# A fused attention and feed-forward kernel on one core: how the second half's four groups of keys are summed in the front attention

## What is computed

```python
B, S, E, H, P = ...          # 4, 1024, 128, 16, 256 here
scores = jnp.einsum('bhid,bhjd->bhij', q, k)
rel = jnp.einsum('bhid,pd->bhip', q, rel_key)
bias = jnp.take_along_axis(rel, jnp.broadcast_to(rel_idx[None, None], (b, h, s, s)), axis=3)
logits = jnp.where(causal[None, None], (scores + bias) * scale, -jnp.inf)
attn = jax.nn.softmax(logits, axis=-1)
out = jnp.einsum('bhij,bhjd->bhid', attn, v)
```

## Time and profile before

| what | value |
|---|---|
| median of 3 runs | 4309.09 us |
| profiled execution, its own time | 4309.43 us |
| its span, first to last instruction | 4307.6 us |
| mean granted clock of TensorE | 0.977 of full speed |
| busy share PE / DVE / ACT / POOL | 96% / 82% / 85% / 56% |
| PE matmul instructions | 44016 |
| steady part of the front attention | about 130 us to 910 us, one head every 12.58 us |

### The profile page before, as it was taken

One profiled execution on the slowest core, in us unless ns is written; L12 is line 12 of the kernel. 1 busy time (PEld: TensorE's weight loads), 2 busy tenths in 40 slices (PEclk: granted clock), 3 DMA queues, 4 the chain that ended last, 5 costly groups with the idle time before them and its releaser, 6 DMA issues. The chain is left out here.

```text
span 4307.6 us, 124384 instructions
## 1 busy us (share of the span) xinstructions
PE 4136.7 (96%) x44016; PEld 2959.0 (69%) x44016; DVE 3537.9 (82%) x8236; ACT 3655.4 (85%) x6994; POOL 2391.7 (56%) x2876
## 2 busy tenths in 40 slices
PE   4999999997999999999999999999999999999995
PEld 2566666654777777777777777777777777777774
DVE  4788888866888888888888888888888888888884
ACT  4899999966888888888888888888888888888885
POOL 3000000026676766767767777677776776766763
PEclk7999999988999999999999999999999999999997
DMA  6777777731111111111111111111111111111111
GB/s 179 226 229 233 228 234 227 237 128 40 36 42 47 42 37 43 42 47 42 36 44 42 45 43 36 44 42 42 47 36 44 42 42 47 36 41 45 42 47 51
DMA packets 249884, 347.66 MB, mean 81 GB/s; under 512 B 45120, under 2 KB 206508, under 8 KB 249260
## 3 DMA queue, kind: packets, MB, share of 16 engines
q1 hardware_dynamic: 249388, 341.00, 26.6%
HBM read 151.13 MB, written 82.85 MB: 54 GB/s over the span
## 5 line engine op out<-in xcount | busy, mean ns | idle before, releaser
L1459 PE MATMUL la_ps<-la_Wqkv,la_xsT 128*128 128x512 f32 x2304 | 1191.0, 612 | 3.4 <-DVE X L1175 2.8
L1175 DVE TENSOR_TENSOR X<-la_ps,la_tab 128x1024 f32<-128x1024 f32 x768 | 919.9, 1218 | 100.2 <-ACT la_sq L1317 97.1
L1122 POOL TENSOR_TENSOR la_rt<-la_rt,la_rn 128x1024 f32<-128x1024 f32 x384 | 722.3, 1902 | 27.5
L1105 POOL TENSOR_TENSOR la_rt<-X 128x512 f32<-128x512 f32 x384 | 494.9, 1289 | 263.0 <-PE la_ps L1474 165.8
L1182 DVE TENSOR_REDUCE la_ssum<-la_sq 128x8 f32<-128x512 f32 x768 | 502.4, 674 | 0.0
L1106 POOL TENSOR_TENSOR la_rt<-X 128x512 f32<-128x512 f32 x384 | 497.2, 1295 | 0.0
L1494 PEld LDWEIGHTS la_ps<-la_kT,la_qB 128*64 128x64 f32 x12288 | 390.5, 138 | 145.8 <-issue 145.8
L1317 ACT ACTIVATE la_sq<-la_ps 128x512 f32<-128x512 f32 x768 | 448.7, 596 | 45.1 <-PE la_ps L1459 30.5
L1459 PEld LDWEIGHTS la_ps<-la_Wqkv,la_xsT 128*128 128x128 f32 x2304 | 377.0, 190 | 142.8 <-issue 93.7
L528 POOL COPY at_vh<-V 128x64 f32 (+1 forms) x64 | 15.1, 236 | 784.5 <-PE at_ps L727 783.3
L1525 PEld LDWEIGHTS la_ps<-la_Wo,la_oT 128*128 128x128 f32 x3072 | 366.6, 192 | 110.4 <-issue 101.2
(11 more groups left out here) (204 smaller groups left out, 9524.7 us busy)
## 6 DMA issues: line engine op xcount, KB each, us to landing
at_band<-skew_scratch SPq DMA_DIRECT2D x64, 1536.0 KB, 7.3
la_vs<-la_v SPq DMA_DIRECT2D x192, 384.0 KB, 3.5
skew_scratch<-at_R SPq DMA_DIRECT2D x64, 1024.0 KB, 6.6
la_vs<-la_v SPq DMA_DIRECT2D x192, 128.0 KB, 3.4
la_Wqkv<-in_wqkv SPq DMA_DIRECT2D x28, 384.0 KB, 3.7
at_qh<-qt_scratch SPq DMA_DIRECT2D x64, 144.0 KB
at_kh<-kt_scratch SPq DMA_DIRECT2D x64, 144.0 KB
la_W<-in_L_ffn_W SPq DMA_DIRECT2D x24, 341.0 KB, 3.7
```

The source lines that it names most:

```text
L1105: e.tensor_tensor(dst[:, :, 0, :], c[:, :, 0, :], s[:, :, 1, :], ALU.add)
L1122: e.tensor_tensor(heads(rt, w), heads(rt, w), wide(rn[:, w * H:(w + 1) * H], D), ALU.mult)\
L1175: e.tensor_tensor(dst.rearrange("p f (h d) -> p f h d", d=D), ps[:, c % 2, :].rearrange("p (h d) -> p h d", d=D).unsqueeze(1).to_broadcast ...
L1459: e.matmul(ps[:, c % 2, :], xsT[:, m * P:(m + 1) * P], Wqkv[:, ds(layer(n) % 2, 1), c * 512:(c + 1) * 512], start=True, stop=True)\
```

## The change

In the second half (u = 1) `gather` no longer multiplies with `sel`. It makes four plain 128x128 transposes of `part` into bank 7, so that each query has its four strips side by side on its own partition. `over_sum` for u = 1 begins with a VectorE reduction that adds the four strips from PSUM (128 x 36 sums of four) into a new SBUF tile `total`. The reciprocal waits for the reduction and reads `total`, and so does the multiplication. The mark `on` is now raised by the reduction, and the multiplication raises a new one, `c_tot`, for which nobody waits. The first half (u = 0) does what it did.

```diff
-        rc, cell = t.sb("rc", [P, G]), t.sb("cell", [P, TB])
+        rc, cell, total = t.sb("rc", [P, G]), t.sb("cell", [P, TB]), t.sb("total", [P, G, D_A + 1])
...
-        c_on = t.mark("co", JJ)
+        c_on, c_tot = t.mark("co", JJ), t.mark("ct")
...
             def over_sum(n, m, u):
-                o = ps[:, O_BANK, 0:G * (D_A + 1)].rearrange("p (i d) -> p i d", i=G)
+                tile, col = n // H_A * TB + G * u, n % H_A * D_A
+                out = O[:, ds(tile, G), ds(col, D_A)]
                 e.wait_ge(g_mm.sem, g_mm.v(n, u + 1))
-                e.reciprocal(rc[:].unsqueeze(2), o[:, :, D_A:D_A + 1]).then_inc(c_on.sem, 1)
-                e.wait_ge(c_on.sem, c_on.v(n, u + 1))
-                tile, col = n // H_A * TB + G * u, n % H_A * D_A
-                e.tensor_tensor(O[:, ds(tile, G), ds(col, D_A)], o[:, :, 0:D_A], wide(rc[:], D_A), ALU.mult)\
-                    .then_inc(on.sem, 1)
+                if u == 0:
+                    o = ps[:, O_BANK, 0:G * (D_A + 1)].rearrange("p (i d) -> p i d", i=G)
+                    e.reciprocal(rc[:].unsqueeze(2), o[:, :, D_A:D_A + 1]).then_inc(c_on.sem, 1)
+                    e.wait_ge(c_on.sem, c_on.v(n, 1))
+                    e.tensor_tensor(out, o[:, :, 0:D_A], wide(rc[:], D_A), ALU.mult).then_inc(on.sem, 1)
+                else:
+
+                    groups = ps[:, O_BANK, :].rearrange("p (i c d) -> p i d c", i=G, c=G)[:, :, 0:D_A + 1, :]
+                    e.tensor_reduce(total[:], groups, AX.X, ALU.add).then_inc(on.sem, 1)
+                    e.wait_ge(on.sem, on.v(n))
+                    e.reciprocal(rc[:].unsqueeze(2), total[:, :, D_A:D_A + 1]).then_inc(c_on.sem, 1)
+                    e.wait_ge(c_on.sem, c_on.v(n))
+                    e.tensor_tensor(out, total[:, :, 0:D_A], wide(rc[:], D_A), ALU.mult).then_inc(c_tot.sem, 1)
...
             def gather(n, m, u):
                 e.wait_ge(o_ev.sem, o_ev.v(n, u + 1))
                 for i in range(G):
-                    k = WIN * min(G, G * u + i + 1)
-                    mm = e.matmul(ps[:, O_BANK, i * (D_A + 1):(i + 1) * (D_A + 1)],
-                                  part[0:k, i * P:(i + 1) * P], sel[0:k, :], start=True, stop=True)
+                    if u == 0:
+
+                        k = WIN * (i + 1)
+                        mm = e.matmul(ps[:, O_BANK, i * (D_A + 1):(i + 1) * (D_A + 1)],
+                                      part[0:k, i * P:(i + 1) * P], sel[0:k, :], start=True, stop=True)
+                    else:
+                        mm = e.transpose(ps[:, O_BANK, i * P:(i + 1) * P], part[:, i * P:(i + 1) * P], ident[:])
                 mm.then_inc(g_mm.sem, 1)
```

## The result

The changed kernel takes 4331.32 us (median of four runs, 4327.58 to 4332.62), the kernel before 4309.46 us beside it: 21.9 us more, a ratio of 1.0050 with a 95% interval of 1.0038 to 1.0062. The profiled execution took 4332.29 us of its own, with a span of 4330.5 us.

What follows compares the result with a forecast made beforehand. The prediction took the chain `scores(7)`, DVE, `values(0)` as the bound, not PE's 98.5%. The DVE chain grows by 0.31 + 0.05 = 0.36 us, times 61 heads 22 us: 4309.1 + 22 = 4331 us, 8-in-10 range 4319 to 4349.

Steps and rivals of the forecast that it cites:

- The median: Whole kernel: 4331 us forecast, 0.5% slower than before; chance 0.77.
- What bounds: Each head: PE work from `values(0)` to `scores(7)`, about 10 us, plus a DVE chain of 2.4 us.
- PE's saving counted at nothing: `gather(1)`, 0.81 to 0.44 us: the 0.37 us saved per head is lost waiting at `rel(2)` and `values(0)`.
- The reduction: DVE chain before the reciprocal: 144 elements from PSUM take 0.31 us, bounds 0.29 and 0.69.
- The wait on itself: DVE, reciprocal waiting for the reduction: 0.05 us, with 0.24 as other end; free by the skill page.
- Reciprocal and multiplication: DVE, behind the reduction: reading SBUF in place of PSUM, both counted as unchanged.
- The number of heads: Of 64 heads, 61 counted because the first few are less regular; 61 x 0.36 = 22 us.
- no slack waits there to take up the delay: Behind `values(0)` or `least(0)` on PE, DVE and ACT: nothing absorbs the 0.36 us per head.
- PE as the bound: Rival: PE's saved 0.37 us per head counts, kernel gets faster by up to 23 us, 4286 us; chance 0.05.
- something takes up the delay: Rival: ACT or DVE is last later in the head, leaving under 0.14 us per head, say 4312 us; chance 0.07.
- A dear stride: Rival, reduction or its wait costs more: badly read stride 0.69 us, 0.74 per head with short wait, 4354 us; chance 0.10.
- the rival of the falling clock: Rival: transposes replacing products drop PE's clock to 1.2 GHz, some 700 us longer, about 5000 us; chance 0.01.

Runs made afterwards that it cites:

- transposes-only run: Changed kernel without the reduction: reciprocal and multiplication read the first of four strips from PSUM; 4305.6 us beside 4306.1 for the kernel before, ratio 0.9998.
- the two kernels with the loads first: Kernel before and changed kernel, each with query and key loads issued ahead of the band's load on SP: 4296.6 us (0.9976) and 4324.8 us (1.0038).
- reduction-only run: Kernel before, products kept, plus the reduction over bank 7 into unused `total` and a wait for it: 4334.5 us beside 4306.1, ratio 1.0059.

## Why the prediction was right

**The median** was forecast as 4331 and is 4331.3 us. The mechanism is the one that was forecast; that the two numbers agree within 1 us is in part luck, as the number of heads shows below.

**What bounds.** The prediction took the chain `scores(7)`, DVE, `values(0)` for the path and PE's 98.5% for no bound. The two halves of the change, each alone, show it: taking work from PE beside the chain gave a ratio of 0.9998, and adding the reduction to the chain alone gave the changed kernel's head.

**PE's saving counted at nothing.** Right, and the place where it is lost was named: `rel(2)`, waiting for ACT's copy. The size of the saving, 0.37 us, was met (0.81 to 0.43 or 0.44). What the prediction did not see is that a little of it can cover the waits for loads: 2.6 us in the trace of the transposes-only run.

**The reduction.** 0.31 us forecast, 303 ns measured. **The wait on itself.** 0.05 us forecast; 521.11 - (520.78 + 0.303) = 0.03 us measured. By the Trainium skill ("VectorE: DVE Perf Modes", The DRAIN you can't avoid), where a semaphore after each operation costs nothing extra, the prediction would have said 4328. The times alone do not decide between the two, since the executions lie between 4327.58 and 4332.62; the traces speak against the page here, since by the estimate above the instruction that waits starts 0.11 us later than one that does not. The prediction took the end of one record as the earliest start of the next, but records can overlap by 0.08 us, in its own rows too: `least(7)` ends at 512.08 + 0.62 = 512.70, and the reciprocal starts at 512.62. Its sum is not touched by this, because it counted the length of the reduction plus the gap behind it. **Reciprocal and multiplication** out of SBUF take 178 and 192 ns, as out of PSUM. Together 0.34 us against 0.36.

**The number of heads.** 61 times 0.36 us made 22. In detail it was 63 heads and other terms: 63 x 0.336 = 21.2 us, and 1.6 us for a pause that every fourth head pays (15 x 0.11), together 22.8, which the two kernels with the loads first confirm (22.9). Between the kernels as they are the stage grew by only 818.7 - 799.5 = 19.2 us, since the kernel before spent about 3.7 us more on waits for loads, which longer heads cover (799.5 - 795.0 = 4.5 before, 818.7 - 817.9 = 0.8 after). That no slack waits there to take up the delay was thus not quite true. The span of the profiled executions grew by 22.9 us: 3.8 us more are behind the stage, in code that the change did not touch, and the stage began 0.2 us earlier. Over all kernels of the table this rest lies between 3388.5 and 3397.9 us, with no order that I can name. It stays open, and it means that the last few microseconds of the agreement are luck: the same change between the two kernels with the loads first made 4324.8 - 4296.6 = 28 us of the medians.

**The rivals.** PE as the bound fell with the transposes-only run. That something takes up the delay is true for 3.7 of 22.9 us, far from the whole, and it was the waits for loads and not ACT. A dear stride fell with 303 ns. The granted clock stayed at 1.00 in the changed kernel with 40 transposes a head, so the rival of the falling clock fell too. By the Trainium skill ("TensorE: Matmul & The Clock Gate", Part 4: PE-mode transpose), where transposes do not count as busy for the clock in the same way, four more of them would speak for a fall. None came here, and the only trace whose clock fell inside the stage, the reduction-only run's, is of a kernel that kept its products. That transposes count for less than products is neither shown nor ruled out by this, since products ran beside them in every head.

## What to carry to other kernels

An engine that is 98.5% busy need not be the bound: look for the place where it waits once per turn, and for the place where the engine it waits for waits in turn. Here work added between these two places cost its full length, and work saved beside them gave next to nothing, so read the two halves of such a trade separately. When a change frees a buffer earlier, move what no longer has to stand before the release out of the chain; here this turned 22 us lost into 11 us gained. And try a second change on the kernel before as well: the order of the loads looked like the next bound behind that gain, but it gave some 10 us to the kernel before too.

## What the runs showed of the hardware

**The granted clock fell in two heads of one trace.** In the run with the reduction only, the granted clock fell twice inside the stage. PE's row where it fell the first time, then a stretch around the second time and PE's rows there:

```profile
276.82 1.80 PE L731 MATMUL at_ps<-at_pT,at_vh 128*32 128x512 f32 x8 [0.63 <-DVE at_pT L565]
...
690.00:695.00 5.00, 4.38 (x31) 2.25 (x29) 3.40 (x15) 4.64 (x9) 0.18 (x1) 0.84 0.33 67
...
693.38 1.91 PE L731 MATMUL at_ps<-at_pT,at_vh 128*32 128x512 f32 x8 [0.62 <-DVE at_pT L565]
...
695.52 1.06 PE L716 MATMUL at_ps<-ident,at_probs 128*128 128x128 f32 x4
696.37 0.60 PE L705 MATMUL at_ps<-at_kh,at_qh 72*128 72x512 bf16 x1
```

Both times PE had just waited 0.62 or 0.63 us before `values(0)`. That is not the usual wait of this kernel, which is 0.51 us, but the longer one of every fourth head. Then four transposes took 0.85 us instead of 0.44, the value of the lower level of 1.2 GHz, and the head took 14.7 us instead of 13.09. In 200 to 900 us this trace has 13 such longer waits, and 11 passed without a fall; the changed kernel and the changed kernel with the loads first have 14 each, all without one. So it is not shown that the wait made the clock fall, only that the two falls stand behind it; if it did, idle time put on PE can cost more than its own length. Whether other executions of the changed kernel had such heads the times alone don't say.

**A pause of 0.105 us on DVE** comes once per turn of the loop at a fixed place in the stream of instructions. In the kernel before and in the one with the transposes only it stands behind the copy that `values(0)` needs, and costs nothing that can be seen: the fourth head is 0.06 us longer than the others (12.64 us), and so it is where the pause is not at this place at all (12.98 against 12.92). With the reduction and its wait added it stood ahead of the copy (13.09), and with one more instruction a head it was harmless again (12.98, in one execution). What makes the pause, the fetching of instructions or something else, was not tried.
